# Attention's written order: measured lengths, changes of tile mode counted, V products in twos

## The reference

```python
x = _layernorm(x + _L0_attn_ref(x, ...))     # 16 heads of 32, causal, gated scores
x = _layernorm(x + _L0_xattn_ref(x, ctx, ctx, ...))   # retention with decay
x = _layernorm(x + _L0_ffn_ref(x, ...))      # quantized gated FFN
```

```python
Q, K, V = (x @ w.T + b).reshape(b, l, h, hd).transpose(0, 2, 1, 3)
scores = where(causal, -1e9, Q @ K.T / sqrt(hd)) * head_gates   # gates from the mean of x
out = softmax(scores) @ V
return out @ wo.T + bo
```

## Time and profile before

| | us |
|---|---|
| median of 3 runs | 1857.51 |
| lowest and highest run | 1852.74, 1859.90 |
| span of the profiled execution | 1854.0 |
| TensorE busy | 1693.4 (91%) |
| VectorE busy | 1387.5 (75%) |
| ScalarE busy | 1049.5 (57%) |
| GpSimd busy | 1042.0 (56%) |

### The profile page before, as it was taken

One profiled execution on the slowest core, in us unless ns is written; L12 is line 12 of the kernel. 1 busy time (PEld: TensorE's weight loads), 2 busy tenths in 40 slices (PEclk: granted clock), 3 DMA queues, 4 the chain that ended last, 5 costly groups with the idle time before them and its releaser, 6 DMA issues. The chain is left out here.

```text
span 1854.0 us, 37186 instructions
## 1 busy us (share of the span) xinstructions
PE 1693.4 (91%) x13426; PEld 763.6 (41%) x13426; DVE 1387.5 (75%) x3039; ACT 1049.5 (57%) x1861; POOL 1042.0 (56%) x1001
## 2 busy tenths in 40 slices
PE   5998999999999999998787999999999998899996
PEld 2433344433433344333233455545455554444432
DVE  7687756777577856688744878878778777788798
ACT  5346555665556655566642556565465454555577
POOL 4049867677775976869872654555555555000044
PEclk9999999999999999999898999999999999899999
DMA  8302112231012311222224223232232131651265
GB/s 274 116 18 61 53 31 58 68 92 42 24 53 78 103 31 25 84 60 81 80 80 164 64 84 101 93 98 97 86 96 88 60 107 47 236 203 46 81 261 187
DMA packets 123039, 172.02 MB, mean 93 GB/s; under 512 B 22376, under 2 KB 73064, under 8 KB 121960
## 3 DMA queue, kind: packets, MB, share of 16 engines
q1 hardware_dynamic: 117336, 160.91, 27.0%
q10 hardware_dynamic: 5520, 8.73, 1.5%
HBM read 106.12 MB, written 38.14 MB: 78 GB/s over the span
## 5 line engine op out<-in xcount | busy, mean ns | idle before, releaser
L1148 DVE CUSTOM_DVE_ANT_0 a_mx<-a_mx,a_mqk 128x128 f32<-128x128 f32 (+3 forms) x512 | 242.0, 511 | 130.7 <-PE a_mx L1348 129.6
L960 ACT ACTIVATE a_P<-a_mx 128x512 f32<-128x512 f32 (+3 forms) x441 | 199.2, 496 | 150.7 <-PE a_mx L1366 80.4
L1231 POOL TENSOR_TENSOR a_P<-a_P 128x512 f32<-128x512 f32 (+3 forms) x202 | 194.2, 990 | 107.7 <-PE a_o L1378 94.6
L1362 PE MATMUL a_mx<-a_Qs,a_Ks 128*128 128x512 f16 (+3 forms) x768 | 231.3, 334 | 19.2 <-ACT a_P L960 7.5
L1348 PE MATMUL a_mx<-a_Ks,a_Qs 96*128 96x512 f16 (+3 forms) x768 | 226.3, 331 | 9.8 <-DVE a_nm L1148 3.0
L960 ACT ACTIVATE share<-a_mx 128x512 f32<-128x512 f32 (+3 forms) x327 | 144.9, 490 | 105.8 <-PE a_mx L1366 59.1
L1231 POOL TENSOR_TENSOR a_P<-a_P,share 128x512 f32<-128x512 f32 (+3 forms) x199 | 184.5, 957 | 27.2 <-ACT share L960 17.4
L1151 DVE TENSOR_REDUCE a_nm<-a_mx 128x1 f32<-128x512 f32 x256 | 164.8, 683 | 31.3 <-PE a_mx L1348 30.4
L2260 PE MATMUL r_pj<-share,cth 128*128 128x512 f16 x672 | 169.6, 386 | 3.6 <-PEq L123 2.7
L2260 PE MATMUL r_pj<-r_xTh,share 128*128 128x512 f16 x512 | 158.9, 383 | 4.4 <-DVE r_xTl L2106 3.7
L3008 PE MATMUL f_pj<-f_xqT,f_wgu 128*128 128x512 bf16 x704 | 158.6, 382 | 0.6 <-DVE f_xqT L2892 0.6
(11 more groups left out here) (302 smaller groups left out, 3999.9 us busy)
## 6 DMA issues: line engine op xcount, KB each, us to landing
x_scratch<-rows SPq DMA_DIRECT2D x60, 256.0 KB, 2.3
rows<-x_scratch SPq DMA_DIRECT2D x56, 256.0 KB, 4.5
lead<-in_xT SPq DMA_DIRECT2D x24, 512.0 KB, 4.4
lead<-in_ctxT SPq DMA_DIRECT2D x38, 256.0 KB, 2.8
h_scratch<-f_h SPq DMA_DIRECT2D x3, 2816.0 KB, 9.1
f_h<-h_scratch SPq DMA_DIRECT2D x3, 2816.0 KB, 9.8
a_Ks<-a_kph SPq DMA_DIRECT2D x256, 32.0 KB, 1.9
a_Qs<-a_qph SPq DMA_DIRECT2D x256, 32.0 KB, 1.9
```

Source lines behind the costliest of these rows:

```text
L960: act.activation(Pf[pf.at[key]][:, off:512], pb[:, off:512], ACT.Exp).then_inc(p_exp, 1)
L1148: dve.tensor_tensor_reduce(bank_of(it)[:, 0:n], bank_of(it)[:, 0:n], mqk[:, 512 - n:512], 1.0, -3e38, ALU.add, ALU.max, nm[:, col:col + 1] ...
L1231: pool.tensor_tensor(total[:, off:512], total[:, off:512], Pf[pf.at[key]][:, off:512], ALU.add).then_inc(add_pool, 1)
L1362: m = pe.matmul(pb[:, off:512], Ks[s][:, j, kt * P:(kt + 1) * P], Qs[s][:, j, qb * 512 + off:(qb + 1) * 512], start=True, stop=not diag)
```

## The change

It touches the planner alone. Every instruction of the kernel stays; the order in which the engines start them is another.

- `Flow.start` adds `TURN`, 0.11 us, to a TensorE item whose kind of tile differs from that of the item before it. `flow.tiles` gives the kinds: `pv`, `sum` and `maxend` are 32 wide, all others aren't. Other phases give none.
- `pick_pe`: a `pv` or `sum` may start at once only when the mode is 32 already; a `pv` also when two `pv` stand in `V`, when it is the last of its half, or when all but one P buffer are taken. Held back, it starts when nothing else can.
- `product` of `qk` starts only when the previous unit's stacks of the same half are done, that of `wo` only when its residual row is in.
- `flow.rank`: `norm` last on VectorE, `qk` first on VectorE and ScalarE, exponentials first on ScalarE.
- New lengths for nearly all kinds.

```diff
@@ Flow.start
+        if engine == "PE":
+            length += TURN * (self.tile != self.tiles.get(item[0]))
+            self.tile = self.tiles.get(item[0])
+TURN = 0.11
+GROUP = 2
@@ attention_plan
-    flow.alone = ("splitx", "nwlo")
+    flow.rank = {("DVE","norm"):2,("DVE","qk"):0,("ACT","qk"):0,("ACT","sc"):0}
+    flow.alone, flow.tiles = ("splitx", "nwlo"), {"pv": 32, "sum": 32, "maxend": 32}
@@ product (three pieces)
-        pe_item(stream, places[1], parts[1], 0.98, None)
+        pe_item(stream, places[1], parts[1], 0.87, None)
@@ qk
-        product(Q, places, "qk", key, lambda: has(("splitx", b), ("splitw", "w" + n)), made)
+        product(Q, places, "qk", key, lambda: has(("splitx", b), ("splitw", "w" + n)) and (
+            not u or has(*(("stack", u - 1, n, hf, j) for j in range(4)))), made)
@@ wo
-        product(W, places, "wo", (b, qb, k), lambda: has(*(("out", 4 * b + g, qb) for g in range(4)), ("splitw", "wo")), mm)
+        product(W, places, "wo", (b, qb, k), lambda: has(*(("out", 4 * b + g, qb) for g in range(4)), ("splitw", "wo"), ("res", b, qb, k)), mm)
@@ maxima
-        pe_item(M, place, work, 0.000458 * n,
-                lambda: put("DVE", work, 0.07 + 0.00104 * n + (0.18 if qt // 4 == hf else 0.0), out, lambda: not u or has(("nm2", u - 1))),
+        pe_item(M, place, work, 0.003 + 0.000417 * n,
+                lambda: put("DVE", work, 0.075 + 0.00104 * n + (0.035 if qt // 4 == hf else 0.0), out, lambda: not u or has(("nm2", u - 1))),
@@ score, pv, add, sums
-            put("ACT", work, 0.08 + 0.00083 * n, out, lambda: room(pf), lambda: pf.take(key))
+            put("ACT", work, 0.05 + 0.00087 * n, out, lambda: room(pf), lambda: pf.take(key))
-        pe_item(S, place, work, 0.000458 * n + (0.06 if kt >= 4 * qb else 0.0), made,
+        pe_item(S, place, work, 0.003 + 0.000417 * n + (0.056 if kt >= 4 * qb else 0.0), made,
-        pe_item(V, u, ("pv", u, qb, kt), 0.15 + 0.06 + 0.00183 * n, made,
+        pe_item(V, u, ("pv", u, qb, kt), 0.03 + 0.00168 * n, made,
-        pe_item(V, u, work, 1.15, made, lambda: bank_ok("sum"), lambda: take_bank(work), 0.35)
+        pe_item(V, u, work, 0.88, made, lambda: bank_ok("sum"), lambda: take_bank(work), 0.35)
@@ pick_pe
-        kept = set()
+        kept, held_back = set(), None
+        waiting = [first[1][0] for first in V if first[1][0][0] == "pv"]
         for first in V:
-            kind, ok = first[1][0][0], first[1][3]
-            if kind not in kept and ok():
-                V.remove(first)
-                return first[1]
-            kept.add(kind)
+            item, ok = first[1][0], first[1][3]
+            if item[0] not in kept and ok():
+                if item[0] not in ("pv", "sum") or flow.tile == 32 or item[0] == "pv" and (
+                        len(waiting) >= GROUP or item[3] == 4 * item[2] + 3 or len(pf.busy) + 2 > pf.n):
+                    V.remove(first)
+                    return first[1]
+                held_back = held_back or first
+            kept.add(item[0])
...
+        if best is None and held_back:
+            V.remove(held_back)
+            return held_back[1]
```

More of the change, by code:

```diff
@@ L137, in __init__ @@
         self.alone, self.last, self.until, self.yields = (), None, 0.0, {}
+        self.tiles, self.tile = {}, None
     def put(self, engine, item, length, end=None, ok=None, begin=None, tail=0.17):
@@ L257, in product @@
         parts = [(f"{kind}.0", *key), (f"{kind}.1", *key), work]
-        pe_item(stream, places[0], parts[0], 0.98, None, lambda: bank_ok(kind) and ok(), lambda: take_bank(work))
-        pe_item(stream, places[1], parts[1], 0.98, None)
-        pe_item(stream, places[2], parts[2], 0.98, end)
+        pe_item(stream, places[0], parts[0], 0.87, None, lambda: bank_ok(kind) and ok(), lambda: take_bank(work))
+        pe_item(stream, places[1], parts[1], 0.87, None)
+        pe_item(stream, places[2], parts[2], 0.87, end)
     def qk(u, n, hf, places):
@@ L307, in made @@
             if (b, qb) == FINAL:
-                put("DVE", work, 0.75, lambda: give_bank(work), lambda: has(("res", b, qb, k)))
+                put("DVE", work, 0.72, lambda: give_bank(work), lambda: has(("res", b, qb, k)))
             else:
-                put("DVE", work, 1.75, out, lambda: has(("res", b, qb, k)) and (not ahead or has(("wonorm", *ahead))))
+                put("DVE", work, 1.6, out, lambda: has(("res", b, qb, k)) and (not ahead or has(("wonorm", *ahead))))
         def out():
@@ L322, in scale @@
             for i in range(4):
-                put("ACT", ("woout", b, qb, i), 0.65, lambda i=i: scaled(i))
+                put("ACT", ("woout", b, qb, i), 0.7, lambda i=i: scaled(i))
         def scaled(i):
@@ L352, in made @@
                 done.add(bank)
-                put("ACT", bank, 0.75, lambda: (give_bank(bank), after(1.3, lambda: done.add(("neg", u)))),
+                put("ACT", bank, 0.9, lambda: (give_bank(bank), after(1.3, lambda: done.add(("neg", u)))),
                     lambda: not u or has(("neg", u - 1)))
-            V.insert(0, (u, (bank, 0.1, made, lambda: bank_ok("maxend"), lambda: take_bank(bank), 0.25)))
-        pe_item(M, place, work, 0.000458 * n,
-                lambda: put("DVE", work, 0.07 + 0.00104 * n + (0.18 if qt // 4 == hf else 0.0), out, lambda: not u or has(("nm2", u - 1))),
+            V.insert(0, (u, (bank, 0.06, made, lambda: bank_ok("maxend"), lambda: take_bank(bank), 0.25)))
+        pe_item(M, place, work, 0.003 + 0.000417 * n,
+                lambda: put("DVE", work, 0.075 + 0.00104 * n + (0.035 if qt // 4 == hf else 0.0), out, lambda: not u or has(("nm2", u - 1))),
                 lambda: bank_ok("max") and has(("stack", u, "q", qt // 4, j), ("stack", u, "k", hf, j), "init"),
@@ L409, in out @@
                 sums(u, qb)
-        put("POOL" if kind == "add.p" else "DVE", (kind, *key), 0.12 + 0.00212 * n if kind == "add.p" else 0.15 + 0.0012 * n, out,
+        put("POOL" if kind == "add.p" else "DVE", (kind, *key), 0.14 + 0.00212 * n if kind == "add.p" else 0.15 + 0.0012 * n, out,
             lambda: kt == 1 or has(("add", u, qb, j, kt - 1)))
@@ L419, in made @@
                 pf.give((u, qb, j, 0))
-            put("DVE", ("norm", u, qb), 3.0, normed, lambda: has(("oc", u, qb)))
+            put("DVE", ("norm", u, qb), 3.15, normed, lambda: has(("oc", u, qb)))
         def normed():
```

## The result

The changed kernel runs in 1852.14 us (median of 12 runs, 1847.34 to 1857.54) against 1857.29 before, a ratio of 0.9972 with a 95% interval of 0.9959 to 0.9986.

The account below looks back on a forecast made before the run. TensorE, busy 581.6 of 602 us in the middle, was taken as the bound. Merges 16.3 + lengths 5 = 21.3 us off the 1854.0 span gives 1832.7, and 3.5 to the median gives 1836; range 1820 to 1858.

Parts of the forecast that it names:

- Value 0 in the middle: Middle units: holding V products for pairs costs nothing, covered by 18 P buffers and GpSimd's free 26%; bounds -2 to +10.
- VectorE has 30% free, so 0: Attention: putting the five-instruction normalization last on VectorE costs 0; from 810 to 897 us perhaps 0 to +4.
- Rival (1): From 110 us on, turns are given back as P buffers become the limit, or not saved: 1856 us, chance 0.20.
- sign of 15: Sign of being wrong: ScalarE's waits for GpSimd, 5.7 us before, at 15 or more.
- signs of being wrong: As many 128x32 stretches; ScalarE's waits at 15; TensorE idle above 25; GpSimd awaiting V products late, tail over 87 us.
- Turns: Attention on TensorE: pairing V products saves 71 merges at 0.23 us, 16.3 us with the ends' merges half counted.
- Clock: Middle: some 6 us are lost in low-clock spells, left as they are, 4 us either way.
- Lengths and ranks: Measured lengths gain 5 us of TensorE's 20.4 idle in the middle; ranks on ScalarE and VectorE 0.
- Start: First 110 us: the bank conditions were taken as 0, from -4 to +4.
- The last two units: Last unit: with 10 P buffers only about 2 merges, 0.5 us gained.
- The rest: The two phases behind the attention stay at 870 us, 2 us either way.
- Rival (3): Units 0, 1, 14, 15: held-back V products delay additions, buffers and exponentials, 29 us lost: 1873 us, chance 0.10.

Follow-up runs that it names:

- yield: The changed kernel, same order, with GpSimd waiting until the layer norm's small VectorE reciprocal and product are done: 1834.7 us (0.9885).
- mrscalar: The changed kernel, same order, no pause, the small product written as four one-column operations with a per-partition scalar: 1836.6 us (0.9898).
- group1: The changed kernel with GROUP = 1 alone, so V products start without pairing, and no pause of GpSimd: 1870.1 us (1.0072).
- lenonly: The kernel before with the measured lengths and nothing else: 1857.2 us (0.9994).
- yield_consts: The kernel of yield, with the first key copy also waiting in the plan for the constants, at 25.5 us: 1828.1 us (0.9856).
- yc_tail20: The kernel of yield_consts, with last-unit additions given to VectorE at a GpSimd backlog 2 us longer, in place of 4: 1825.4 us (0.9829).
- yc_nobank: The kernel of yield_consts without the two new start conditions, of `qk` and of `wo`: 1851.0 us (0.9974).

## Why the prediction was wrong, step by step

The saving that the forecast rests on came (fewer changes of tile mode, at the price read from the rows); the time was wrong, since a cost was missing. With the product out of GpSimd's way the same order takes 1834.7 or 1836.6 us; 1836 was forecast. That this agrees is luck: in yield the middle gained 31 us, where 18 were forecast (13.3 for merges, 5 for lengths), while the start and the last two units lost 8 and 6, where 3 were to be gained.

- **The step that failed** is the cover of what the pairing and the new order cost: "Value 0 in the middle" for the pairs, since GpSimd has 26% free, and "VectorE has 30% free, so 0" for the ranks. Each engine's free time was looked at alone, and not whether a VectorE operation can run while GpSimd does. In its place the runs showed two spells, 7.42 and 7.91 us, in which VectorE was shut out; taking them away is worth 17 to 19 us (mrscalar, yield). The pairs aren't needed for them (group1 has three); which part of the change brings the product into a chain of additions stays open.
- **Rival (1)** has the time "given back", but by P buffers, and that did not happen: ScalarE's waits for GpSimd in the middle are 14.5 us in 18 pieces, all under 1.7. The 5.7 us of the earlier trace rows, against which the prediction sets its sign of 15, is one row alone; all such waits from 208 to 810 us are 9.1 us, and over the twelve units 11.1, so 3.4 were added. Of the signs of being wrong one did come: TensorE idle above 25 us in those units (35.5). It was 25.5 there before the change already.
- **The rows of before showed the collision.** Additions on VectorE took 1.77 and 1.50 us beside GpSimd, where alone they take 0.68, at 923.1 and 926.7. And in the earlier trace rows, VectorE is busy all of 400 to 402 us with one instruction, a split with two SBUF inputs that takes 1.22 us alone:

```profile
399.38 2.83 DVE L1007 SCALAR_TENSOR_TENSOR share<-lead,share 128x1024 f16<-128x1024 f32 x1
```

  Another took 2.84 at 621.0. Behind each of the two the clock stood at 0.50 for 6.8 us, from 401.4 and 623.3 on. The prediction read only the clock off. Whether the split caused that stall isn't shown: TensorE waited 1.2 us for an exponential, then 0.6 for the maximum behind the split.
- **What VectorE collided with.** The Trainium skill ("SBUF — State Buffer", Who interferes with whom) says that a VectorE instruction with two SBUF inputs contends with a GpSimd instruction that reads SBUF. All spells agree, and so does the one-input form. The same page of the Trainium skill (Summary: rules for kernel authors) says that the second to issue blocks until the first finishes; here the measurement differs: VectorE lost to eight additions in a row.
- **Turns**: 16.3 us forecast for 71 merges. 67 came, 61 of them in the middle, where 58 were forecast. At full clock in the trace of before a block of 512 columns alone takes 1.094 us from due time to the next start (median of 69), two together 1.953 (14), so a merge saves 0.235, and as much at 128 and 256 columns (0.454 and 0.667 alone, 0.884 together). That makes some 15.7 us, an estimate from these rows: the term was right. The lower price of 0.11, which the prediction also worked out, is not what the trace shows.
- **Clock**: the prediction left the some 6 us that low clock costs in the middle as they are. The clock stood at 0.50 there for 17 us before and never in yield; at half the speed that is up to 8.5 us, an estimate, and a good part of the middle's 31. The merges are 14 and the shorter idle time (25.5 to 20.2 us) 5 of it; the remaining 3 or so are open.
- **Lengths and ranks**: 5 and 0 forecast, 24 and 38 when left out of the full change, banks 23 with 0 forecast. These don't add up (with the pairs' 8 they are 93, and the whole is 29): each part left out breaks an order that the others fit, and lenonly shows that the lengths alone give nothing. The forecast's term for lengths was read from the idle time of one order, and idle time is not what another order costs. So which part of the 29 us is due to which term is not shown, but for the turns.
- **Start**: no term had it. The 0 from -4 to +4 for the first 110 us was for the bank conditions, and the ranks were priced 0 there; putting the key copy first cost some 6 us (yield_consts gets 6.5 back), by a transfer that the planner doesn't know.
- **The last two units**: 0.5 us gain forecast, 6 lost (137 to 143, also in yield). Before, seven additions of the last unit went to VectorE, after none; giving seven back (yc_tail20) recovers 1.5 of it in the profile. The rest stays open.
- **The rest**: 870 forecast, 866.
- **Rival (3)** would have cost 29 us at both ends; TensorE's waits for exponentials before V products in the last two units, its mark, are 12.7 us after and 11.3 before, so at most a small part of it came.

What decides whether VectorE loses to one addition or to eight stays open. Of the products that began beside a running addition some waited for that one alone (0.65 to 0.93 us), also inside a chain, and I found no rule in their timing.

## What to carry to other kernels

Before writing or changing an order by hand or by planner, list the VectorE operations with two SBUF tensor inputs and look at what GpSimd does beside them; one on a chain that others wait for gets a pause of GpSimd, or a form with a scalar or PSUM operand in place of the second, however small it is. Free time of two engines is a cover only if they can use it at once. In this kernel measured lengths were worth nothing without the conditions around them, and the parts of a planner can't be priced one at a time from the idle time of the old order. What a plan doesn't know (a transfer's landing, a shared port) is where its order fails: compare the plan's first wait of each engine with the chip's.

## What the runs showed of the hardware

- A VectorE operation with two SBUF inputs was shut out by up to twelve GpSimd additions in a row (9.2 us in yield), for up to 9.8 us (nine of them, yc_nobank), whatever its size (4 columns, 7.9 us). The 16 that stood for 5 us or more got in when GpSimd paused; others lost to a single addition and got in between two.
- With one input in SBUF and one in PSUM, 546 splits beside GpSimd all took 0.67 to 0.69 us.
- The same arithmetic with a per-partition scalar in place of the second tensor: 0.203 to 0.215 us in all 28 places.
- A change to 128x32 tiles and back costs TensorE 0.235 us in the timeline (1.094 alone, 1.953 for two), and 0.21 us by experiment (9.6 us for 46 in the middle twelve units).
